# Tail projections in four 32-token column tiles, and the turn of the maxima as a plain product

## The reference, cut to what matters

```python
dots = jnp.einsum('bhid,bhjd->bhij', q, k) * scale
attn = jax.nn.softmax(dots, axis=-1)
out = jnp.einsum('bhij,bhjd->bhid', attn, v)
out = out.transpose(0, 2, 1, 3).reshape(b, n, dim)
return out @ w_out + b_out              # then t = t + this
...
logits = flat @ Wr                      # flat: the layernorm of t; the experts' choice
```

## Time and profile before

| what | us |
|---|---|
| median of 3 runs | 1181.38 (1180.64 to 1184.5) |
| the profiled execution | 1179.94, span 1177.8 |
| PE busy | 1095.2 (93%) |
| PE weight loads busy | 742.7 (63%) |
| DVE busy | 817.8 (69%) |
| ACT busy | 629.4 (53%) |
| POOL busy | 602.2 (51%) |
| second attention batch, 392 to 504 us | PE 107.07, DVE 91.87, ACT 76.12, POOL 70.67 |

### The profile page before, as it was taken

How to read it: one execution, slowest core, us unless ns; L and a number is a source line. 1 busy time by engine, 2 the same in 40 slices (tenths; PEclk the granted TensorE clock), 3 DMA queues, 4 the chain that set the end, 5 groups by cost and what they waited for, 6 DMA issues and landing times.

```text
span 1177.8 us, 34627 instructions
## 1 busy us (share of the span) xinstructions
PE 1095.2 (93%) x13416; PEld 742.7 (63%) x13416; DVE 817.8 (69%) x1493; ACT 629.4 (53%) x1144; POOL 602.2 (51%) x513
## 2 busy tenths in 40 slices
PE   7999999978899999999999989899999999999995
PEld 4464645434455555555555545688989989999883
DVE  4666666666688888788878882768655656655773
ACT  3566575546577657766776665453333333333332
POOL 3425241314788763776486546167645544543540
PEclk9999999999799999999999999999999999999998
DMA  5255842625223231434153213823333323322328
GB/s 174 90 176 209 320 163 79 198 72 186 58 62 84 88 83 31 103 96 107 53 130 96 57 48 97 309 38 78 57 50 56 46 47 55 51 44 44 47 38 290
DMA packets 98908, 121.00 MB, mean 103 GB/s; under 512 B 29024, under 2 KB 76064, under 8 KB 98112
## 3 DMA queue, kind: packets, MB, share of 16 engines
q1 hardware_dynamic: 75280, 70.40, 20.0%
q0 software_dynamic: 20400, 42.08, 15.4%
q10 hardware_dynamic: 3072, 6.30, 1.5%
HBM read 73.10 MB, written 45.47 MB: 101 GB/s over the span
## 4 chain that ended last, share of the span: by engine, by line
PE 66%; DVE 15%; DMA 6%; issue 6%; DVEq 2%; ACT 2%; POOL 1%; SPq 1%; POOLq 0%; ACTq 0%
PE PP L1023 21%; PE PP L1450 11%; PE PP L1335 7%; DVE mxp L1741 7%; PE PP L1307 6%; PE PP L1194 4%; PE PP L1122 3%; PE PP L1254 3%; PE PP L1039 3%; DMA res_d<-WORK,lb 2%; PE PP L1317 2%; PE PP L1322 2%; PE PP L1154 1%; DVE WORK L2019 1%; DMA WORK<-v_d 1%
## 5 line engine op out<-in xcount | busy, mean ns | idle before, releaser
L953 ACT ACTIVATE WB<-PP 128x512 f32<-128x512 f32 x512 | 268.8, 604 | 143.2 <-PE PP L1335 143.2
L1741 DVE TENSOR_REDUCE mxp<-PP 128x2 f32<-128x1024 f32 x242 | 287.0, 1219 | 63.3 <-PE PP L1254 62.7
L993 ACT ACTIVATE WORK<-PP,b1c 128x256 f32<-128x256 f32 (+1 forms) x320 | 139.6, 450 | 236.6 <-PE PP L1023 198.3
L699 POOL TENSOR_TENSOR WB<-WB 128x1024 f32<-128x1024 f32 x84 | 198.6, 2365 | 87.0 <-PE PP L1322 58.0
L782 POOL DMA_INDIRECT res_d<-WORK,lb x70 | 117.9, 1684 | 154.4 <-DVE WORK L2036 141.3
L1450 PE MATMUL PP<-WB,WORK 128*128 x1704 | 193.1, 273 | 0.0
L1023 PE MATMUL PP<-WORK,WB 128*128 128x256 f16 (+1 forms) x1552 | 175.8, 273 | 2.4 <-DVE WORK L2005 1.7
L1450 PEld LDWEIGHTS PP<-WB,WORK 128*128 128x128 f16 x1704 | 164.6, 98 | 19.6 <-issue 0.2
L1023 PE MATMUL PP<-WORK 128*128 128x128 f16 (+6 forms) x1086 | 161.2, 300 | 10.6 <-DVE WORK L1658 3.6
L1335 PE MATMUL PP<-WORK 97*32 97x256 f16 x4096 | 163.1, 279 | 7.2 <-ACT WB L953 4.3
L1023 PEld LDWEIGHTS PP<-WORK,WB 128*128 (+1 forms) x1552 | 152.5, 102 | 21.6 <-issue 4.5
(11 more groups left out here) (319 smaller groups left out, 1199.8 us busy)
## 6 DMA issues: line engine op xcount, KB each, us to landing
WORK<-in_L_ffn_W_dram POOLq DMA_DIRECT2D x32, 512.0 KB, 4.0
res_d<-WORK SPq DMA_DIRECT2D x8, 1024.0 KB, 4.6
late_d<-WB POOLq DMA_DIRECT2D x1, 6144.0 KB, 19.3
WB<-late_d ACTq DMA_DIRECT2D x3, 2048.0 KB, 14.1
v_d<-WORK SPq DMA_DIRECT2D x4, 1024.0 KB, 5.6
WORK<-q_hi_d SPq DMA_DIRECT2D x16, 256.0 KB, 3.7
WORK<-v_d SPq DMA_DIRECT2D x8, 512.0 KB, 6.2
WORK<-k_hi_d SPq DMA_DIRECT2D x16, 256.0 KB, 3.8
```

Of the source, the lines that this page charges most:

```text
L699: pool.tensor_tensor(PS[n % 2], PR[n % 3][:, 0], PR[n % 3][:, 1], ALU.add).then_inc(s("pair_kept"), 1)
L953: act.activation(PR[n % 3][:, c // 2, c % 2 * 2:c % 2 * 2 + 2], SCORES[m % 3] .rearrange("p (h n) -> p h n", h=2), ACT.Exp).then_inc(s("e_ ...
L993: act.activation(hid[:, k, 0:width], hidden_bank(k)[:, 0:width], ACT.Gelu, bias=b1c[:, bass.ds(e, 1), k], scale=1.0 / WSCALE)\
L1741: dve.tensor_reduce(mxp[:, n // 4 % 2, i, h:h + 2, k], PP[2 + h // 2][:, :].rearrange("p (h n) -> p h n", h=2), X_AXIS, ALU.max).then_inc( ...
```

## The change

The turn of the maxima becomes an ordinary product with the identity, no longer a transpose; its output is the same 8 x 128. The projection of 128 tokens is no longer two products with 128-column weights: for each half of the channels, four products follow each other, each with the weights of 32 tokens, each writing its own 32 partitions of the same bank, and the second half adds to the first. The moving operand of the four is the same. The semaphore is raised by the last. All waits and the place of both in the order stay. The first turn, before the loop (L1168), and the other transposes are untouched.

```diff
                 bank = next_slot(b, before)
                 pe.wait_ge(s("nm_kept"), b * UNITS + (u + 1))
-                pe.transpose(bank[0:2 * GH, 0:P], mx[:, :], identf[:, :]).then_inc(s("c_made"), 1)
+                pe.matmul(bank[0:2 * GH, 0:P], mx[:, :], identf[:, :], start=True, stop=True).then_inc(s("c_made"), 1)
 
...
             def tail_project(t, b, before, n):
...
-                tok_at = slice(t * P, (t + 1) * P)
-                product(bank[:, 0:WIDE], [(OS[:, k, tok_at], wo_sb[:, k]) for k in range(CC)], "c_made")
+                for k in range(CC):
+                    for r in range(P // D):
+                        mm = pe.matmul(bank[r * D:(r + 1) * D, 0:WIDE], OS[:, k, t * P + r * D:t * P + (r + 1) * D],
+                                       wo_sb[:, k], start=(k == 0), stop=(k == CC - 1), skip_group_check=True)
+                mm.then_inc(s("c_made"), 1)
```

## The result

The changed kernel took 1167.11 us in the median of 6 runs (1165.50 to 1173.24), against 1182.41 (1180.64 to 1184.50) of the kernel before in the same comparison: a ratio of 0.9883, 95% interval 0.9854 to 0.9912. The forecast was 1172.4 with a range from 1169.0 to 1178.5. Two more sets of six executions of the changed kernel had medians of 1169.47, inside the range, and 1167.88. The mean of all 18 is 1168.4; that of 88 executions of the kernel before, from the four later comparisons, is 1180.5. That is 12.1 us apart. Within the three comparisons that had both kernels the means are 13.8, 12.1 and 14.5 us apart, 13.5 on average. The gain to be explained is thus 12 to 13.5 us, each with an uncertainty of about 0.8, where 9.0 was forecast.

What follows compares the result with a forecast made beforehand. PE was taken to bound the kernel, with DVE close behind in attention steps. Terms 6.0 + 1.75 - 0.2 + 1.4 = 9.0 us off the median 1181.38 gave 1172.4 us, range 1169 to 1178.5.

Steps and rivals of the forecast that it cites:

- The bound and the loop: Attention loop: PE sets projecting steps, DVE close behind; 32-token tiles gain 0.25 us in each of 24 projections, 6.0 us.
- The rival that loads in line would cost 18 us: Projections: weight loads of the four tiles do not overlap, 0.58 us lost in each of 32, +18.6 us; chance 0.04.
- The turn: Turn of the maxima as plain product: 0.22 us for 0.31, gain 0.09 in 16 of 31 turns, 1.4 us.
- the loop has 6.8 to 7.1 for 7.4: Attention loop: 7.4 us forecast, 6.0 from 24 projections and 1.4 from the turns.
- The rival with the full tile: Turn of the maxima: eight columns keep the full tile, +3.5 us in 16 turns, time 1177.3 us; chance 0.12.
- The last six projections: End of the attention stage, no maxima to wait for: five give 0.31 us each, the sixth perhaps 0.2, together 1.75.
- the two projections in the expert tile: Last two projections, between 128*128 products in the first expert tile: two added changes of shape, cost 0.2 us.
- 6.0 + 1.75 - 0.2 + 1.4 = 9.0 us: Whole gain: loop projections 6.0, last six projections 1.75, two in the expert tile -0.2, turns 1.4.
- the lowest rival, 1171.0: Loop: DVE never binds, all 0.31 us a projection arrive, 7.4 in place of 6.0, sum 10.4 us; chance 0.08.
- the spread of a median: Whole time: allowance that, with both rivals near 1177.4, made the range 1169 to 1178.5 us.

Runs made afterwards that it cites:

- e7: The changed kernel with PE's five register loads ahead of the experts moved into the last five attention steps; ratio to the kernel before 0.9884, mean 1165.9 us.
- e12: The kernel before with PE's five register loads ahead of the experts moved into the last five attention steps; ratio to the kernel before 0.9989.
- e4: The kernel before, unedited, run once more as a measure of the spread; ratio 1.0006, mean 1180.5 us.
- e3: The changed kernel, unedited, run once more for a second trace; ratio to the kernel before 0.9905, mean 1168.8 us.
- e14: The changed kernel, unedited, run a third time beside other variants; ratio to the kernel before 0.9877, mean 1167.7 us.
- e15: The same kernel as e7, run again beside the changed kernel; ratio to the kernel before 0.9876, mean 1166.9 us.
- e5: The changed kernel with one small useless 128*128 product (f16, 8 columns) ahead of each projection outside the first expert tile; ratio to the kernel before 1.0012.
- e9: The kernel before with one small useless 128*128 product (f16, 8 columns) behind each transpose of the maxima; ratio to the kernel before 0.9994, mean 1178.5 us.
- e13: The changed kernel with 32 useless score-shaped products in each of three waits for DVE, moving the instruction fetch; ratio to the kernel before 0.9916, mean 1172.2 us.

## Why the prediction was right and wrong

**The bound and the loop: right.** PE set the projecting step, by a little, and now DVE does. The chain of numbers held at almost each point: 0.43 and 0.89 (forecast 0.43 and 0.89), 1.32 from the sums to the scores (1.32), DVE 0.15 ahead of the maxima (0.14), the step 3.63 (3.63). That the step came out to the hundredth is partly luck: DVE reads at 1.57 after the sums, not at "about 1.5", so only 0.19 was gained behind the sums and not 0.25, and 0.06 came ahead of the sums, where nothing was forecast. 24 x 0.242 = 5.8 against 6.0. The rival that loads in line would cost 18 us is ruled out. The Trainium skill's rule in "TensorE: Matmul & The Clock Gate", section "The mechanism", that a load overlaps running matmuls only when its row group differs, taken by itself, does not hold for this form: the sixteen loads of the projection's tiles share their rows of the array and last about 110 ns each, 1.76 us together, and their matmuls are issued within 0.89 us (406.97 to 407.86).

**The turn: the sum right, the way there not.** Eight columns count as a 32-column tile, and the two passes follow each other at 0.11 us. But the scores were to start 0.65 after the sums, and they start at 0.44, since scores of other tiles run beside the passes. On PE the turn thus costs 0.11, not 0.22. What arrived was 0.095 in each of nine projecting steps (0.09) and 0.10 to 0.11 in six turn steps, 1.5 us against 1.4. With the small losses in the other steps the loop has 6.8 to 7.1 for 7.4. The rival with the full tile fell.

**The last six projections: a step that failed, the other way.** "Five pass on all, 5 x 0.31 = 1.55; the sixth ends the stage and gives perhaps its 0.2" asked what is late next on DVE's side and not on PE's own sequencer. The register loads behind the last projection were already late by 1.20 us in the profile of before, as "issue", and faster matmuls only uncover them (about 0.9 us); behind the longer pause the lower clock came in five of six traces and took 2.2 us more. With the two projections in the expert tile, 0.9 us were lost where a gain of 1.55 was forecast. e7 against e12 shows 2.0 once the loads are away, so the size of the saving itself was about right.

**What the sum did not have: the step that put the time under the range.** The sum "6.0 + 1.75 - 0.2 + 1.4 = 9.0 us" counted the change's own operations and put all else at nothing, without a reason. Two things outside it moved. The instruction fetch met the scatter of the list less: 2.2 us (78.5 on the mean of before and e4, 76.3 of after, e3 and e14), or 1.5 with e12, e7 and e15 counted in (78.1, 76.6). And the steps behind the long waits kept the upper clock more often in these traces: 1.3 us, with a cause that is not shown. From the traces, then: some 7 + 1.5 to 2.2 + 1.3 - 0.9, about 9 to 9.5 of 12 to 13.5. That this is near the forecast 9.0 is luck, since terms that it did not have stand in for one that it had with the wrong sign.

The other 3 to 4 us are not in these pieces. The traced executions differ less than the others: their spans average 1175.5 us (before, e4) and 1167.2 (after, e3, e14), 8.3 apart, and the two traced executions of the kernel before, 1179.94 and 1174.95, lie 3 us under its mean of 1180.5 on average. What its slower executions have is open.

**The range: too narrow below.** 1169 lies 2 us under the lowest rival, 1171.0, and that was left for "the spread of a median". Nothing was left for effects outside the change, though the profile of before already showed them: an instruction fetch in a 4.1 us wait for 32 small packets, and the lower clock behind all three long waits, 1.0 to 1.4 us each. With some 3 us for them, an estimate from these rows, the range would have begun near 1166.

## What to carry to other kernels

A short product between others is cheapest in its neighbours' tile shape: the small full-tile product of e5 cost 0.22 us in a step that PE sets, and even 64-column tiles paid for the difference. Before forecasting a gain at the end of a stage, read "issue" gaps as work of the engine's own sequencer, here register loads of 0.73 us each, and place those loads early. Treat any change in the number of instructions as able to move a time-critical small DMA against an instruction fetch, and give that 2 to 3 us of range on its own: here the seven tiles took 75.7 to 77.5 us without the meeting and 79.1 to 79.6 with it.

## What the runs showed of the hardware

- An f32 product with 8 weight columns runs beside products of other 32-column tiles (starts 0.01 us apart), where the f32 transpose of the same data stood alone: 0.54 after the sums, with the scores 0.74 after them. e9 shows that the transpose already pays for the full shape: with a full-tile product of 8 columns right behind it (427.99 after 427.88) the scores still start 0.74 after the sums (428.09 after 427.35). The Trainium skill lists the f32 transpose among what column tiling disables ("TensorEngine Tiling (Array Packing)", section "Restrictions"), which fits.
- One instruction fetch of 16 KB within the wait for a scatter of 32 packets, 2.8 to 3.1 us behind the first piece, went with a wait of 3.8 to 4.3 us in place of 2.0 in three traces of three, and with seven expert tiles about 3 us longer; the third of them, e13, had been built to bring this about. How the one delays the other is not shown.
- After the same pause of 1.80 us the next 16 matmuls went at 1.2 GHz in one execution of a kernel and at 2.4 GHz in another. Which, differed between kernels with 32-token projections (15 of 18 at the upper clock) and with full-tile ones (8 of 21).
